# A graph layer's sorted edge tiles: the last chunk laid end to end, 416 tiles gathered and their rows copied by VectorE

## What is computed

```python
edge_in = concat([h[row], h[col], dist])        # 53125 edges, h is 3125 x 64
e = silu(edge_in @ eW1 + eb1)                   # 128 wide
e = silu(e @ eW2 + eb2)
agg = segment_sum(e, row, num_segments=3125)
out = silu(concat([h, agg]) @ nW1 + nb1) @ nW2 + nb2
result = layernorm(h + out)
```

## Time and profile before

| what | value |
|---|---|
| median of three runs | 629.5 us (628.17 to 629.7) |
| profiled execution, span | 629.0 us |
| profiled execution, time of its own | none given beside the span |
| PE busy | 530.9 us, 84% |
| VectorE busy | 463.5 us, 74% |
| GpSimd busy | 429.0 us, 68% |
| ScalarE busy | 355.5 us, 57% |
| gathers (L736) | 440, 953 ns mean |

### The profile page before, as it was taken

How to read it: one execution, slowest core, us unless ns; L and a number is a source line. 1 busy time by engine, 2 the same in 40 slices (tenths; PEclk the granted TensorE clock), 3 DMA queues, 4 the chain that set the end, 5 groups by cost and what they waited for, 6 DMA issues and landing times.

```text
span 629.0 us, 15166 instructions
## 1 busy us (share of the span) xinstructions
PE 530.9 (84%) x4653; PEld 447.6 (71%) x4653; DVE 463.5 (74%) x1364; ACT 355.5 (57%) x812; POOL 429.0 (68%) x465
## 2 busy tenths in 40 slices
PE   4942869879879989998998899889997888879795
PEld 3421658768768869887887778778776777769684
DVE  6987999988999899989888869797642533223356
ACT  5842555455555556755655555565556666656464
POOL 2337576566777777777777777777777777777750
PEclk9986899779999999999999999999999999999997
DMA  5211111111111121111121111111111121111111
GB/s 121 77 51 51 43 52 48 36 50 48 56 52 52 52 56 56 52 56 49 54 56 52 51 55 56 53 52 55 54 54 55 52 56 54 53 55 53 55 39 51
DMA packets 17215, 34.17 MB, mean 54 GB/s; under 512 B 8133, under 2 KB 9352, under 8 KB 17142
## 3 DMA queue, kind: packets, MB, share of 16 engines
q0 software_dynamic: 14080, 28.86, 16.0%
q1 hardware_dynamic: 2594, 3.40, 2.1%
q10 hardware_dynamic: 468, 0.96, 0.6%
HBM read 30.73 MB, written 2.40 MB: 53 GB/s over the span
## 4 chain that ended last, share of the span: by engine, by line
POOL 32%; DVE 25%; PE 21%; issue 16%; DMA 3%; DVEq 1%; SPq 0%; POOLq 0%
POOL q_rows L736 32%; PE layer_ps L749 9%; PE sort_ps L749 6%; PE seg_ps L749 5%; DVE load_hot L1212 3%; DVE agg L1283 3%; DVE count L1058 2%; DMA q_rows<-q_table,q_index 2%; DVE hot L1268 2%; DVE col_hot L1206 1%; DVE row_hot L1207 1%; DVE place L1102 1%; PE turn_ps L841 1%; DMA src_i<-in_src_dram 1%; DVE slot L1108 1%
## 5 line engine op out<-in xcount | busy, mean ns | idle before, releaser
L736 POOL DMA_INDIRECT q_rows<-q_table,q_index x440 | 419.4, 953 | 159.5 <-issue 127.6
L583 ACT ACTIVATE e<-layer_ps 128x512 f32<-128x512 f32 x110 | 65.7, 597 | 212.7 <-PE seg_ps L749 204.3
L1283 DVE TENSOR_TENSOR agg<-agg,seg_ps 128x125 f32 x416 | 93.3, 281 | 93.5 <-PE seg_ps L749 90.3
L749 PE MATMUL layer_ps<-hotT,p_table 128*128 128x128 bf16 x1320 | 158.8, 225 | 0.2
L749 PE MATMUL layer_ps<-ident_f,q_rows 128*128 128x128 f32 x440 | 126.7, 288 | 33.6 <-DMA q_rows<-q_table,q_index 32.8
L749 PE MATMUL seg_ps<-hot,e 128*128 128x125 f32 x880 | 125.1, 286 | 23.9 <-DVE agg L1283 23.9
L749 PEld LDWEIGHTS layer_ps<-hotT,p_table 128*128 x1320 | 122.3, 98 | 22.7 <-issue 2.3
L749 PEld LDWEIGHTS seg_ps<-hot,e 128*128 128x128 f32 x880 | 109.5, 196 | 27.3 <-issue 25.3
L749 PE MATMUL layer_ps<-w_sb,h 128*128 128x128 f32 x880 | 119.5, 279 | 0.0
L749 PEld LDWEIGHTS layer_ps<-w_sb,h 128*128 128x128 f32 x880 | 111.2, 193 | 4.6 <-issue 0.2
L749 PEld LDWEIGHTS layer_ps<-ident_f,q_rows 128*128 128x128 f32 x440 | 63.0, 143 | 44.3 <-DMA q_rows<-q_table,q_index 43.3
(11 more groups left out here) (193 smaller groups left out, 439.9 us busy)
## 6 DMA issues: line engine op xcount, KB each, us to landing
q_rows<-q_table,q_index POOLq DMA_INDIRECT x440
q_table<-q_in_sb SPq DMA_DIRECT2D x1, 784.0 KB
x_sb<-in_x_dram ACTq DMA_DIRECT2D x1, 700.0 KB
q_table<-q_in_sb SPq DMA_DIRECT2D x1, 616.0 KB
out_dram<-x_sb SPq DMA_DIRECT2D x2, 224.0 KB
out_dram<-x_sb SPq DMA_DIRECT2D x1, 252.0 KB
w_in<-in_edge_weight_dram SPq DMA_DIRECT2D x1, 185.9 KB
dst_i<-in_dst_dram SPq DMA_DIRECT2D x1, 185.9 KB
```

Of the source, the lines that this page charges most:

```text
L583: A.activation(e2[:, m % 2, :], e_of(m)[:], ACT.Silu).then_inc(e2_ready, 1)
L736: P.indirect_dma_start(q_rows[:, g % RING, j, :], None, q_table, bass.IndirectOffsetOnAxis(ap=q_index[:, GT * g + j:GT * g + j + 1], axis= ...
L749: return nc.tensor.matmul(o, lhsT, rhs, start=start, stop=stop, **kw)
L1283: D.tensor_tensor(o, o, seg_ps[:, j * LO:(j + 1) * LO], ALU.add).then_inc(agg_added, 1)
```

## The change

1. The last chunk has no full tiles and flush tiles any more. Its edges and all that was carried (25 windows' leftovers, copied by ScalarE to `kept`) are laid end to end, window after window, over tile borders (`pack`). 53125 edges fill 416 tiles (`FETCHED`). A tile that holds edges of two windows is worked on twice, once for each, so 440 tile-and-window pairs and 110 steps stay, but GpSimd gathers each tile once: 416 gathers.
2. From step 84 (`PACK`) on gathers go to `last_rows`, a ring of 64 tiles (`KEEP`) in SBUF that takes the place of arrays of the sort. VectorE copies each pair's rows from there to `q_rows`, from a place that it reads from a table (`q_at`), as an addition of zeros in PSUM (`place_rows`, four a step). For step m it waits until the gathers up to group m have landed (fixed tile numbers, whatever tile the pair needs); SyncE adds up the 20 groups' semaphores for that.
3. A batch of the last chunk has one more one-hot (`own_hot`, the tile in which the edge lies) and one more product with it. Five batches of the kept edges come new, on 128 partitions; the closing product and `dest_hot` of this chunk go. All its parts move four steps earlier: `MATCH` to step 59, batches to 66 to 78. `READ` stays at 80.
4. `merge` goes. `hidden` multiplies `agg[0]` and `agg[1]`, two products in the place of one.

The diff, cut to its core:

```diff
+LAST = CHUNKS - 1
+FETCHED = -(-EDGES // SLOT)
+FETCHES = FETCHED // GT
+PACK = SURE[LAST - 1] // GT
+KEEP = 64
@@ plan
-    for k in range(5, CHUNKS):
+    for k in range(5, LAST):
+    k, r = LAST, SURE[LAST - 1] // GT - 8
...
+    steps = [*range(r - 10, r - 1), *range(r - 2, r + 3)]
+    sorts(k, steps, [v + 1 for v in steps])
+    at(VECTOR, r + 4, (READ, k, 0))
@@ SyncE
+            for fetched in last_in:
+                sp.wait_ge(fetched, 16 * GT)
+                sp.sem_inc(landed, GT)
@@ GpSimd
-            for g in range(GROUPS):
+            for g in range(PACK):
...
+            pool.wait_ge(index_ready, CHUNKS)
+            for i, fetched in enumerate(last_in):
+                if GT * (i + 1) > KEEP:
+                    pool.wait_ge(*first_done(PACK + i + (WIN + GT - 2 - KEEP) // GT))
+                for j in range(GT):
+                    at, t = (GT * i + j) % KEEP * HID, GT * (PACK + i) + j
+                    P.indirect_dma_start(
+                        last_rows[:, at:at + HID], None, q_table,
+                        bass.IndirectOffsetOnAxis(ap=q_index[:, t:t + 1], axis=0)).then_inc(fetched, 16)
@@ PE, first_layer and hidden
-                pe.wait_ge(rows_in[m % RING], 16 * GT * (m // RING + 1))
+                if m < PACK:
+                    pe.wait_ge(rows_in[m % RING], 16 * GT * (m // RING + 1))
+                else:
+                    pe.wait_ge(rows_placed, GT * (m - PACK + 1))
...
-                pe.wait_ge(agg_whole, n + 1)
-                mm(hid_banks[n][:, 0:(b1 - b0) * LO], n1a_sb[:], agg[0][:, b0 * LO:b1 * LO], True, True) \
+                mm(hid_banks[n][:, 0:(b1 - b0) * LO], n1a_sb[:], agg[0][:, b0 * LO:b1 * LO], True, False)
+                mm(hid_banks[n][:, 0:(b1 - b0) * LO], n1a_sb[:], agg[1][:, b0 * LO:b1 * LO], False, True) \
@@ VectorE, sort
+                if k == LAST:
+                    made = mark(D.tensor_tensor(pairs(own_hot[0:p, q, 0:m, :]), iota(OWN), each(owns, OWN), ALU.is_equal))
...
+                if k == LAST:
+                    dve.wait_ge(hots_ready, sum(HOTS[:n]) + 2)
+                    own = [p, m, OWN // 2, 2]
+                    D.tensor_tensor(pairs(load_hot[0:p, q, 0:m, V - 1, 0:OWN]), pairs(own_hot[0:p, q, 0:m, :]),
+                                    values[:, :, V - 1, :].unsqueeze(2).to_broadcast(own), ALU.mult).then_inc(hots_ready, 1)
@@ VectorE, new
+            def place_rows(m):
+                rows = nc.values_load_multi_w_load_instructions(
+                    q_at[0:1, GT * (m - PACK):GT * (m - PACK + 1)], engines=(ENG.DVE,), min_val=0, max_val=(KEEP - 1) * HID,
...
+                dve.wait_ge(*first_done(m - RING))
+                dve.wait_ge(landed, GT * min(m - PACK + 1, FETCHES - PACK))
+                dve.wait_ge(window_read, CHUNKS)
+                for j in range(GT):
+                    D.tensor_tensor(q_rows[:, m % RING, j, :], last_rows[:, bass.ds(rows[j], HID)], zero_c,
+                                    ALU.add).then_inc(rows_placed, 1)
@@ VectorE, main loop
+                if PACK - 1 <= m < GROUPS - 1:
+                    place_rows(m + 1)
-                if n == 0:
-                    merge(0)
-                if n >= 0:
-                    merge(n + 1)
```

More of the change, by code:

```diff
@@ L76, in batches @@
 def batches(k):
-    return [(a, min(BATCH, LOAD[k] - a)) for a in range(0, LOAD[k], BATCH)]
+    left = [(LOAD[k] + b, 5) for b in range(0, WIN, 5)] if k == LAST else []
+    return [(a, min(BATCH, LOAD[k] - a)) for a in range(0, LOAD[k], BATCH)] + left
 MATCH, SCAN, TOTAL, OFFSET, SUM, SLOTS, DEST, WINDOW, SORT, READ, CARRY, CLOSE, ENCODE, NODE_X, RESIDUAL, CARRIED = (
@@ L756, in sort @@
                 pe.wait_ge(hots_ready, sum(HOTS[:n + 1]))
+                p = EP if a < LOAD[k] else 128
+                end = {0: LOAD[0] - 1, LAST: LOAD[LAST] + WIN - 1}.get(k)
                 for b in range(m):
-                    last = mm(sort_ps[k % 2][:, :, 0:c], row_hot[:, n % SORTS, b, :], load_hot[:, n % SORTS, b, :, 0:c],
-                              a + b == 0, k == 0 and a + b == LOAD[k] - 1)
+                    last = mm(sort_ps[k % 2][:, :, 0:c], row_hot[0:p, n % SORTS, b, :], load_hot[0:p, n % SORTS, b, :, 0:c],
+                              a + b == 0, a + b == end)
                 if n in SIGNALLED:
                     last.then_inc(sort_mm, 1)
+                elif k and a + m - 1 == end:
+                    last.then_inc(sorted_ready, 1)
             def part(name, k, i):
@@ L1208, in sort @@
+                if k == LAST:
+                    made = mark(D.tensor_tensor(pairs(own_hot[0:p, q, 0:m, :]), iota(OWN), each(owns, OWN), ALU.is_equal))
+                D.tensor_tensor(pairs(row_hot[0:p, q, 0:m, :]), iota(SLOT), each(rows, SLOT),
                                 ALU.is_equal).then_inc(hots_ready, 1)
                 done(made)
-                if k < MERGED:
-                    wide = [EP, m, V, c // 2, 2]
-                    D.tensor_tensor(load_hot[:, q, 0:m, :, 0:c].rearrange("p m v (a b) -> p m v a b", b=2),
-                                    pairs(col_hot[:, q, 0:m, 0:c]).unsqueeze(2).to_broadcast(wide),
-                                    values.unsqueeze(3).to_broadcast(wide), ALU.mult).then_inc(hots_ready, 1)
-                    return
@@ L1216, in sort @@
-                for v in range(V):
-                    D.tensor_tensor(pairs(load_hot[:, q, 0:m, v, 0:c]), pairs(col_hot[:, q, 0:m, 0:c]),
-                                    each(values[:, :, v, :], c), ALU.mult).then_inc(hots_ready, 1)
+                wide = [p, m, V, c // 2, 2]
+                all_values = D.tensor_tensor(load_hot[0:p, q, 0:m, :, 0:c].rearrange("p m v (a b) -> p m v a b", b=2),
+                                             pairs(col_hot[0:p, q, 0:m, 0:c]).unsqueeze(2).to_broadcast(wide),
+                                             values.unsqueeze(3).to_broadcast(wide), ALU.mult)
```

268 lines of the change are left out of this document (153 added, 115 removed).

## The result

| | before | after |
|---|---|---|
| median of seven runs each | 630.6 us | 634.0 us |
| ratio, 95% interval | | 1.0054 [1.0036, 1.0072] |
| span of the profiled execution | 629.0 us | 629.9 us |
| SyncE done with its last store | 628.8 us | 626.9 us |

The forecast was 628.2 us and "same"; the measured time lies above its range. The last two rows of the table are the puzzle: the last store ended 1.9 us earlier than before, and the span still ended later. (Of the 1.9, 1.15 lie ahead of the part that the forecast is about: group 103's last gather started at 575.46 in this execution and at 576.61 in the one before, a difference between single executions.)

What follows compares the result with a forecast made beforehand. Gathers were taken to set 5.0 us a step from about step 45, PE to bound the end. Gathers -6.7, copies +1.2 and hidden products +4.2 sum to -1.3 us: span 627.7, time 628.2, range 625.2 to 632.5.

Steps and rivals of the forecast that it cites:

- the sum: Effect on the span's end: -6.7 + 1.2 + 4.2 = -1.3 us, giving span 627.7 and time 628.2 us.
- Gathers, -6.7 us: 24 fewer gathers: steps 103 to 106 run at PE's own pace, 15.2 us instead of 21.9.
- Copies, +1.2 us: VectorE's four copies between gather and PE start step 103 1.2 us later, paid once; bounds 0.9 and 2.5.
- Doubled hidden products, +4.2 and 1.1 in step 106: PE multiplies agg[0] and agg[1]: products 2 to 6 add 5 x 0.84 us, step 106's new ones 1.06.
- Rival B: At the end, extra hidden products are half hidden by closing norm work: 2 to 4 us vanish, 624 to 627; 25%.
- VectorE's crowding, 0: More VectorE work while the last chunk is sorted: PE some 5 us late around step 68, cost 0, at most 5.
- Rival C: VectorE too full around steps 66 to 76: lag passes 12 us, GpSimd stops, time 633 at lag 17; 15%.
- Shared port, 0: VectorE's copies, with an operand in PSUM, do not hold up GpSimd's gathers: 0 us.
- Rival D: Copies lock GpSimd: 80 gathers at 0.3 to 0.5 us each, 24 to 40 us, time 652 to 668; 6%.
- rival E: A low PE clock stretch, as over step 106 before (0.71), comes anyway: 1.7 us credit lost, 629.9; 9%.
- Rival F: Fixed numbers hold steps 104 to 109 too, so the gain does not come; chance within Rival C's.
- The base: Time taken as 0.5 us above the profiled span of 629.0, from a three-run median of 629.5.

Runs made afterwards that it cites:

- pool_free: Changed kernel with the norm's first scaling moved from GpSimd to VectorE, so GpSimd has nothing behind its gathers: 631.6 us, ratio 1.0006 to the kernel before.
- after_early_drain: Changed kernel with an explicit GpSimd drain added right behind its last gather: 631.7 us, ratio 1.0014 to the kernel before.
- after_no_drain: Changed kernel with GpSimd's closing drain switched off: 632.0 us, ratio 1.0016 to the kernel before.
- merge_free: Changed kernel with agg[1] added to agg[0] by VectorE again, one hidden product, first scaling moved to VectorE: 627.3 us, ratio 0.9935 to the kernel before.

## Why the prediction was wrong

**The step that failed** is one that was never written down: the sum went from PE to the last store and took that for the span's end. The text said of GpSimd only how it paces the gathers, and the 24 fewer entered as a gain alone. They also changed what GpSimd's closing drain has to work off, 9.8 us instead of 3.2, and that put GpSimd behind SyncE: 2.5 us on the median (1.0054 against 1.0014 with the early drain), about three quarters of the measured loss of 3.4. The views of before showed no sign of it. The drain's record did: 3.2 us, 2.1 without the scaling, where VectorE's takes 0.7.

**Gathers, -6.7 us: right.** Steps 103 to 106 took 15.1 us against the 15.2 of the sum, down from 21.9, at the full clock. Gathers stayed 1.25 us apart.

**Copies, +1.2 us: too small for the one step that counts.** Three rows of the changed kernel show the path from a group's last gather over VectorE's copies to PE's first product:

```profile
545.51 0.94 POOL L781 DMA_INDIRECT last_rows<-q_table,q_index  x1 [0.30 <-issue]
```

```profile
548.21 0.88 DVE L1381 TENSOR_TENSOR q_rows<-last_rows,const_ps 128x128 f32<-128x128 f32 x4 [3.00 <-SPq L492]
```

```profile
549.14 0.33 PE L793 MATMUL layer_ps<-ident_f,q_rows 128*128 128x128 f32 x1 [0.33 <-DVE q_rows L1381]
```

It is 3.6 us here and in most steps, against 2.5 before (576.61 to 579.10): +1.1, with 0.9 for the four copies and 0.2 for the signals. Some steps took longer (4.5 us from 550.50 to 554.99). But the sum needs it at step 103, and there the rows came later:

```profile
579.12 0.88 DVE L1381 TENSOR_TENSOR q_rows<-last_rows,const_ps 128x128 f32<-128x128 f32 x4 [1.61 <-SPq L492]
```

That is 3.66 us behind the gather of 575.46 and not the 2.7 of step 97. The last gather's data landed 3.45 us after its start where others take about 2.5, and so in every trace of the changed kernel and its variants (3.4 to 4.4 us; the same gather in the kernel before and its variants 2.4 to 2.5). It is the one gather whose tile is nearly empty, 5 edges of 128; whether that is the reason was not tested. Step 103 then began 4.6 to 5.5 us behind its last gather in these traces, 2.5 to 2.6 in those of the kernel before: **about +2.1 at least, where the sum has +1.2**. That step 103 began at 580.46 as forecast (580.3), and step 109 at 606.23 (606), is luck: this execution's gathers stood 1.15 us earlier than those of the trace that the sum started from.

**Doubled hidden products, +4.2 and 1.1 in step 106: right.** 1.68 us each in the chain, and 3.4 and 4.3 us from the runs that took them out. Rival B is out.

**VectorE's crowding, 0: right.** PE's lag was larger than forecast, its products of step 69 began 9.7 us behind the last gather instead of 2.5, so 7 us late and not 5, but within the 12 that were free. GpSimd's wait for PE fell from 17.2 to 14.5 us. Rival C is out.

**Shared port, 0: right.** 944 ns in the mean for the last chunk's 80 gathers, none above 950. Rival D is out, and the Trainium skill, page "SBUF — State Buffer", section "SBUF: two separate sides", is agreed with by the 22 of them that lay beside a copy with a PSUM operand.

**The clock, rival E: a low stretch came, but where it cost nothing.** PE's first product of step 98 waited 1.89 us for rows, and the granted clock was 0.86 over the next steps (stretch, length, busy, clock):

```profile
554.99 0.33 PE L793 MATMUL layer_ps<-ident_f,q_rows 128*128 128x128 f32 x1 [1.89 <-DVE q_rows L1381]
```

```profile
554.99:566.79 11.80, 10.06 (x80) 0.86 0.19 52
566.79:580.46 13.67, 13.32 (x132) 1.00 0.20 45
```

It was full again well ahead of step 103, and the gathers set the rhythm there. **Rival F** is out: steps 104 to 106 came at PE's own pace.

**A second, smaller miss.** Without the drain's cost the change measures +0.06, +0.14 and +0.16% (pool_free, after_early_drain, after_no_drain), +0.4 to +1.0 us, where the sum said -1.3: about 2 us are missing. The late step 103 is 1 us of them and more. From group 103's last gather to the start of PE's closing drain the changed kernel and its variants with doubled products take 42.3 to 43.2 us and the kernel before and its variants 42.3 to 43.0, so this part, on which the whole forecast rests, gained next to nothing. The remaining microsecond or less lies within the spread of single executions, whose last gather of group 103 starts anywhere from 575.5 to 579.9 where no drain stands ahead of it. The mean granted clock (0.953 over pool_free's runs, 0.958 over those of before beside it) may have a part in it; that was not tested.

**The base.** I put the time 0.5 us above the span, from the median of three runs. In the runs since it is 1.8 to 1.9 us in nearly all of either kernel, one more microsecond that made 628.2 too low; over seven runs the kernel before has 630.6 and not 629.5. Drain 2.5, second miss 2.2 (by after_early_drain) and base 1.1 make up the 5.8 us between 628.2 and 634.0.

## To carry to other kernels

A sum that stops at the last store is complete only if every engine has reached the closing barrier by then: look at what each engine does last and how long its drain takes, above all for an engine that has issued many gathers. If it has idle time between its last gather and its last instruction, a drain in that idle time costs nothing and took 2.5 us off this kernel. And when a change gains by removing work in one place and pays by doubling work in another, try the halves apart: here the gain with the payment left out, and GpSimd's last instruction moved (merge_free), is 0.65% where the whole was a loss. And a forecast that meets a time in the trace, as here 580.46, is borne out only if its distance from the event that it was worked out from is right too.

## What the runs showed of the hardware

- GpSimd's closing drain is not a fixed cost: 1.26 us (its last instruction included) with no gather since an earlier drain, 7.80 with 80, in both programs, so 82 ns for each; and between 3.2 and 10.4 us with 240 to 440, not growing with the number. In 12 of the 14 drains listed above the excess over the bare one is, to 0.6 us, 82 ns for each gather of the remainder on division by 104 (a remainder of 0 counting as 104); the other two are worth 92 gathers for 240 and 112 for 440.
- A drain inserted amid the gathers held them up: from the last gather ahead of it to the next 4.2 us instead of 1.25 with 336 gathers gone before, 5.6 with 360, 7.6 with 176, 9.6 with 200. The order is that of the remainders 24, 48, 72 and 96.
- The changed kernel's last gather, for a tile with 5 edges of 128, landed 3.4 to 4.4 us after its start in 13 traces, the gather of the same number in the kernel before and its variants after 2.4 to 2.5 in five. Why is not shown.
- The wait at the barrier is put down to PE in the views, although GpSimd ended last.
